# Half of a three-tap filter moved from TensorE to ScalarE and VectorE in a projection stage

## The reference, cut to what matters

```python
q = silu(causal_dwconv(x @ Wq, conv_q))      # 4 taps per channel
k = silu(causal_dwconv(x @ Wk, conv_k))
v = silu(causal_dwconv(x @ Wv, conv_v))
fs = fir(v, fir_short)                       # 3 taps per channel, causal
fl = fir(v, fir_long)                        # 31 taps
```

## Time and profile before

| what | value |
|---|---|
| median of three runs | 2584.63 us |
| lowest, highest | 2580.68, 2588.43 us |
| span of the profiled execution | 2587.5 us |
| the stage `conv_heads` in it | 117 to 442.7 us |
| TensorE, records of matmuls, whole span | 2394.4 us, 93% |
| VectorE, whole span | 1655.0 us, 64% |
| ScalarE, whole span | 1109.5 us, 43% |

### The profile page before, as it was taken

One profiled execution on the slowest core, in us unless ns is written; L12 is line 12 of the kernel. 1 busy time (PEld: TensorE's weight loads), 2 busy tenths in 40 slices (PEclk: granted clock), 3 DMA queues, 4 the chain that ended last, 5 costly groups with the idle time before them and its releaser, 6 DMA issues.

```text
span 2587.5 us, 41994 instructions
## 1 busy us (share of the span) xinstructions
PE 2394.4 (93%) x14594; PEld 1659.7 (64%) x14594; DVE 1655.0 (64%) x4354; ACT 1109.5 (43%) x2350; POOL 616.3 (24%) x417
## 2 busy tenths in 40 slices
PE   6899997667897999979999999999999999999998
PEld 4466665555676888845666666666666666666665
DVE  4487886449922566525767676667667676766675
ACT  2477876346663222224334424433443344244331
POOL 1145554031101111211312231222123132312210
PEclk9999998787667999989999999999999999999999
DMA  5447556978767767421202210220122022101000
GB/s 166 162 149 219 174 166 192 270 212 203 212 155 223 217 204 225 156 74 49 58 1 58 58 50 9 58 58 13 45 59 58 1 58 58 43 15 58 9 9 8
DMA packets 376312, 272.14 MB, mean 105 GB/s; under 512 B 199714, under 2 KB 333794, under 8 KB 373906
## 3 DMA queue, kind: packets, MB, share of 16 engines
q1 hardware_dynamic: 371474, 243.85, 33.6%
q0 software_dynamic: 4640, 25.73, 2.9%
HBM read 168.60 MB, written 100.93 MB: 104 GB/s over the span
## 4 chain that ended last, share of the span: by engine, by line
PE 43%; DVE 9%; issue 3%; POOL 2%; ACT 0%; DMA 0%; DVEq 0%; SPq 0%; POOLq 0%; ACTq 0%
PE mx_dn L2002 16%; PE mx_up L1988 15%; PE mx_m L1938 4%; DVE mx_acc L2316 4%; PE mx_m L1965 2%; POOL mx_rms L1894 2%; PE mx_m L1942 1%; PE mx_m L1979 1%; DVE hl L2224 1%; DVE mx_st L2214 1%; DVE hl L2199 1%; DVE hl L2188 1%; DVE mx_rms L2193 1%; PE mx_m L1973 1%; PE mx_m L1947 1%
## 5 line engine op out<-in xcount | busy, mean ns | idle before, releaser
L2316 DVE SCALAR_TENSOR_TENSOR mx_acc<-mx_dn,mx_comb,mx_acc 128x256 f32<-128x256 f32 x1024 | 424.3, 478 | 356.6 <-PE mx_dn L2002 352.7
L2002 PE MATMUL mx_dn<-mx_edn,mx_hs 128*128 128x256 f32 x2048 | 487.7, 381 | 0.0
L1988 PE MATMUL mx_up<-mx_h2T,mx_eup 128*128 128x512 f32 x1024 | 484.3, 595 | 0.0
L2002 PEld LDWEIGHTS mx_dn<-mx_edn,mx_hs 128*128 128x128 f32 x2048 | 384.4, 190 | 145.6 <-issue 91.0
L2090 ACT ACTIVATE mx_hs<-mx_up 128x512 f32<-128x512 f32 x320 | 190.8, 596 | 625.8 <-PE mx_up L1988 625.1
L1988 PEld LDWEIGHTS mx_up<-mx_h2T,mx_eup 128*128 128x128 f32 x1024 | 190.9, 190 | 156.1 <-issue 145.2
L675 DVE SCALAR_TENSOR_TENSOR cv_acc<-cv_pre,conv_w,cv_acc 128x512 f32<-128x512 f32 x288 | 215.7, 750 | 78.2 <-ACT cv_acc L597 71.3
L539 PE MATMUL cv_pj<-cv_hT,wqkv 128*128 128x512 f32 x384 | 181.8, 604 | 12.7 <-ACT cv_acc L597 7.7
L713 POOL TENSOR_TENSOR rn<-cv_ss,half_pow 128x8 f32 x64 | 127.5, 1992 | 13.2 <-POOL cv_ss L709 13.2
L1880 POOL TENSOR_TENSOR mx_st<-mx_tmp,root_pow 128x24 f32<-128x24 f32 x30 | 124.6, 4168 | 20.1 <-DVE mx_tmp L2142 20.1
L1938 PE MATMUL mx_m<-mx_hT,wr 128*128 128x512 f32 x256 | 122.2, 601 | 3.3 <-DMA mx_x<-_attn_hidden_states_dram 2.5
(11 more groups left out here) (292 smaller groups left out, 3998.7 us busy)
## 6 DMA issues: line engine op xcount, KB each, us to landing
kqT_d<-cv_kqc SPq DMA_DIRECT2D x16, 1024.0 KB, 8.5
vf_d<-cv_vf SPq DMA_DIRECT2D x16, 1024.0 KB, 5.4
fl_toep<-taps_d SPq DMA_DIRECT2D x32, 392.0 KB, 7.3
ds_kqT<-kqT_d SPq DMA_DIRECT2D x10, 1024.0 KB, 5.9
fl_v<-vf_d SPq DMA_DIRECT2D x8, 1216.0 KB
ci_kT<-kqT_d POOLq DMA_DIRECT2D x19, 512.0 KB, 5.7
fl_d<-fl_out POOLq DMA_DIRECT2D x8, 1029.0 KB, 7.2
xin<-_attn_hidden_states_dram SPq DMA_DIRECT2D x16, 512.0 KB, 4.3
```

The lines of the kernel that those rows point to most:

```text
L1988: ins = pe.matmul(up_ps[x % 2][:], lhs, h2T[i][:, k, :], start=(k == 0), stop=(k == KD - 1))
L2002: ins = pe.matmul(dn_ps[(i + n) % 2][:, j, :], hs[x % 4][:, j * P:(j + 1) * P], rhs, start=(x == 0 and j % 2 == 0) or x >= NS, stop=(x >= ...
L2316: ins = dve.scalar_tensor_tensor(out=acc[i][:, j, :], in0=dn_ps[(i + n) % 2][:, j, :], scalar=comb[i][:, j, e:e + 1], in1=acc[i][:, j, :], ...
```

## The change

The short filter of channels 0 to 127 leaves PE. ACT multiplies the tile `vT[:, 0]` by the last tap into a new tile `fsT` (128x512), behind the last Silu of the unit and ahead of the halos. DVE adds the two other taps at the start of its `body`, ahead of the next unit's first block. PE's `turn_v` transposes the finished tile instead of doing three matmuls with the diagonal matrices, and its first turn of a unit waits for it, between the transposes of `vT` and that of `fsT`. Channels 128 to 255 stay as they were. There is one `fsT`, so ACT waits until PE has turned the unit before. The taps `fs_w` now live until the early stages end, and three semaphores are new.

```diff
@@ turn_v, on PE
+                if j == 0:
+                    pe.wait_ge(fsT_done, u + 1)
+                pe.transpose(vf_ps[j % 2][:, D:D + P], fsT[:, c0:c0 + P], m.ident[:])
-                for k in range(KD):
-                    for t in range(FIRS):
-                        ins = pe.matmul(vf_ps[j % 2][:, D + k * P:D + (k + 1) * P], vT[i][:, k, c0 + t:c0 + t + P],
-                                        m.diag_fs[:, k, t, :], start=(t == 0), stop=(t == FIRS - 1))
+                for t in range(FIRS):
+                    ins = pe.matmul(vf_ps[j % 2][:, D + P:2 * D], vT[i][:, 1, c0 + t:c0 + t + P], m.diag_fs[:, 1, t, :],
+                                    start=(t == 0), stop=(t == FIRS - 1))
@@ silu, on ACT
                 act.activation(dst, acc[o % 3][:], ACT.Silu).then_inc(silu_done, 1)
+                if o == NBLK - 1:
+                    act.wait_ge(silu_done, u * NBLK + (NBLK + 2))
+                    if not isinstance(u, int) or u:
+                        act.wait_ge(vf_done, u * J)
+                    act.activation(fsT[:], vT[i][:, 0, FIRS - 1:], ACT.Identity, scale=m.fs_w[:, 0, FIRS - 1:FIRS])\
+                        .then_inc(tap_done, 1)
@@ new, on DVE, and called first in body
+            def short(u, g):
+
+                i = g % 2
+                dve.wait_ge(tap_done, u + 1)
+                dve.wait_ge(vhalo_done, u + 1)
+                dve.scalar_tensor_tensor(out=fsT[:], in0=vT[i][:, 0, 1:1 + UT], scalar=m.fs_w[:, 0, 1:2], in1=fsT[:],
+                                         op0=ALU.mult, op1=ALU.add).then_inc(tap_step, 1)
+                dve.wait_ge(tap_step, u + 1)
+                dve.scalar_tensor_tensor(out=fsT[:], in0=vT[i][:, 0, 0:UT], scalar=m.fs_w[:, 0, 0:1], in1=fsT[:],
+                                         op0=ALU.mult, op1=ALU.add).then_inc(fsT_done, 1)
@@
             def body(u, g, nxt):
+                short(u, g)
                 for s in range(NBLK):
```

More of the change, by code:

```diff
@@ L56, in setup @@
         taus = sb("taus", [P, 8])
-        fs_w = sb("fs_w", [P, KD, FIRS])
+        fs_w = m.fs_w
         fl_w = sb("fl_w", [P, KD, FIRL])
@@ L454, in conv_heads @@
         vT = [sb(f"cv_vT{i}", [P, KD, FIRS - 1 + UT]) for i in two]
+        fsT = sb("cv_fsT", [P, UT])
         kqc = [sb(f"cv_kqc{i}", [P, 2 * KD, UT]) for i in two]
@@ L473, in conv_heads @@
         silu_done = sem("cv_silu_done")
+        tap_done = sem("cv_tap_done")
+        tap_step = sem("cv_tap_step")
+        fsT_done = sem("cv_fsT_done")
         vf_done = sem("cv_vf_done")
@@ L2417, in build @@
             m.wqkv = early.enter_context(nc.sbuf_tensor("wqkv", [P, KD, 3 * D], F32))
+            m.fs_w = early.enter_context(nc.sbuf_tensor("fs_w", [P, KD, FIRS], F32))
             for stage in EARLY:
```

## The result

The changed kernel takes 2603.31 us (median of 7 runs, 2595.71 to 2617.21), the kernel before 2586.35 us (7 runs). The ratio is 1.0066, with a 95% interval from 1.0041 to 1.0092: 17 us slower. The forecast was 2594.0, with a range from 2586 to 2607.

A forecast was written before the change was run, and what follows sets the result against it. The prediction took the ring between DVE and ACT, not PE, as the bound. 15 x 0.58 for ACT's tap less 4.2 gave +4.5 us, clock dips +4.8: +9.3, 2594.0 us, range 2586 to 2607.

The forecast's parts named there:

- The ring of DVE and ACT: Projections stage, unit boundary: DVE waits for ACT's scaled copy, ACT for DVE's last block; sets the period, pause 2.97 us.
- Rival 2: Projections stage: PE is the bound after all, so the kernel gets faster, -17 us, 2568; chance 0.06.
- rival 1: Projections stage: the clock holds everywhere, +4.5 us, 2589.1; chance 0.27.
- PE's relief: PE's lighter turns remove DVE's wait before the last block of a unit: 4.2 us back.
- ACT's tap: Inside the boundary pause, behind the last Silu: 0.58 us a boundary, at 15 boundaries.
- The tail: Stage's end: first turn some 2.2 us later, four turns 0.56 us shorter each; net 0, ends -1 and +1.
- DVE's taps: At the boundary, T+1.3 to T+2.85, inside the pause lasting to T+3.55: cost nothing, 0.7 us to spare.
- Rival 4: Unit boundary: DVE's taps aren't covered because the tap's chain is 0.7 late; +12 us, 2597; chance 0.09.
- PE's pause: First V turn of a unit: PE idles about 1.8 us ahead of the filtered tile, 2.9 of 3.3 us in all.
- The clock: PE's clock dips at 8 of 15 boundaries, 0.5 us each, plus 0.8 for half a longer dip: +4.8 us.
- rival 3: All 15 boundaries dip, a third of them twice as long: +20 us, 2605; chance 0.13.
- one sign of being wrong: The prediction counted itself wrong if, among other signs, another stage moved by over 2 us.

The follow-up runs named there:

- d_pehalf: Kernel before with PE's part of the change alone: one transpose for three filter matmuls, no ACT or DVE work, no wait; 2577.8 us, ratio 0.9956.
- a_fill: Changed kernel plus two idle-filling matmuls on PE in each unit's first V turn, ahead of the wait for the filtered tile; 2597.65 us, ratio 1.0025.
- c_nodve: Changed kernel without DVE's two taps, PE waiting for ACT's tap instead; 2590.55 us, ratio 1.0009.

## Why the prediction was right or wrong

Where the 15.7 us of the stage come from, by differences between profiles. The passages run from T of unit 0, the end of DVE's last block of it, to T of unit 15: 140.0 to 427.6 before, 141.0 to 425.6 in d_pehalf, 138.9 to 428.1 in a_fill, 141.0 to 444.4 after. The tail is what follows up to the long filter. Each kernel needed 19.5 us ahead of the passages.

| difference | 15 passages | tail | stage |
|---|---|---|---|
| PE's part alone (d_pehalf less before) | -3.0 | -2.0 | -5.1 |
| the taps and the wait for the filtered tile, clock held by the fillers (a_fill less d_pehalf) | +4.7 | +2.4 | +7.2 |
| the falls of the clock (the changed kernel less a_fill) | +14.1 | -0.5 | +13.6 |
| all | +15.8 | -0.1 | +15.7 |

The rows add up by construction; what each holds was forecast by itself. The two falls of d_pehalf, some 1.3 us in all, stand in the first row as a loss and in the second as a gain.

- **What bounds.** Right. The ring of DVE and ACT sets the period; 36 us taken from PE gave 5.1. Rival 2 is out, and so is rival 1, as the clock fell at 12 passages.
- **PE's relief.** Right. Forecast 4.2 in the passages; in the 13 of them in which the clock held before and in d_pehalf, 3.8 us were gained, some 4.3 for all 15.
- **ACT's tap.** Forecast 0.58 a passage, 8.7 in all; measured 0.42 on the average of the same 13 passages of d_pehalf and a_fill (5.5 us), some 6 for all 15. The next instruction did start 0.62 behind the tap, but 0.14 came back further on, between the second halo and the copy behind it (0.23 from start to start before, 0.09 after); why is not shown. The 0.5 us that a loop's end added to the ring also vanished under the tap.
- **The tail.** Right: forecast as 2.2 more for the later first turn and 2.2 less for the shorter turns. PE's part alone gave 2.0, the wait took it back, and the whole came to -0.1.
- **DVE's taps.** Right: T+1.3 to T+2.8, with 0.57 to spare, and c_nodve shows the same pause without them (3.42 us). Rival 4 is out.
- **PE's pause.** Right in place: 1.75 us, forecast as 1.8. The idle time ahead of the transposes of `vT` was forecast as 1.1 everywhere; it was 1.06 where the unit before had no fall and 0.37 where it had one, as the last kq turn then ended at T+0.35 and not at T-0.4. So eight of the 12 falls came behind 2.1 us of idle time and not the 2.9 that the forecast worked with.
- **The clock.** The mechanism was right and its size was not: +4.8 forecast, +14.1 measured in the passages (+13.6 in the stage). This is the term that failed, twice. I took 8 passages with a fall; there were 12. And I priced one at 0.5 us by ACT's wait for one kq turn alone; most cost 1.0. The third block started 0.67 late against the unit without a fall, and ACT, which has next to no slack in a slot, came late to the fourth block as well, by 0.31 more (0.59 and 0.23 of idle time on DVE). The two long ones cost 2.2 and 2.3, close to the 2.1 priced (0.5 and 1.6), and there were two where half of one was counted. The ten others cost 0.8 to 1.0. The end of the range, rival 3 (+20 us), was nearer to the truth than the forecast, but partly by luck: it had 15 falls at too low a price and five long ones.
- **By the sum.** 4.5 + 4.8 = 9.3 against 2.1 + 13.6 = 15.7: the first term was 2.4 too high, the second 8.8 too low. The direction was right, and the result lies inside the range because the range was drawn around rival 3.
- **Two readings beside the sum.** The profiled execution before was not the slowest of the three: each run on record lies some 1.7 us above its own span (2599.86 for 2598.1), which puts it near 2589.2, above all three times. Nothing in the sum hangs on it. And one sign of being wrong did come, another stage that moves by over 2 us: the mixing was 4.1 us shorter and the long filter 2.1. Since the mixing also differs by 4.2 us between the two executions of a_fill, that says nothing against the ring; for the long filter no run shows the reason.

## What to carry to other kernels

When work is moved off an engine that looks full, ask first what sets the period, and then what the moved work's wait does to the engine that was relieved: here the lighter TensorE waited in one piece of 1.75 us, its clock fell in 12 of 15 passages, and the half-speed stretch hit the next deadline. Start the moved work where the engines already stand (ACT's idle time ahead of the last Silu), so that its result is there before it is asked for. A filler of idle matmuls is a cheap test that tells a clock loss from a work loss.

## What the runs showed that was not expected

- The clock falls behind pauses that are not whole: 0.37, 0.18 and 1.02 us of idle with transposes and six matmuls between them were enough at seven passages of c_nodve.
- A pause of one and the same size goes with a fall or without. In the changed kernel all four boundaries with 2.7 to 2.8 us of idle time went with a fall, but only eight of the eleven with 2.1 (0.37 and 1.75 ahead of 266 with a fall, 0.38 and 1.75 ahead of 306 without). What decides there is not shown.
- The falls repeat from one execution to the next: the changed kernel's 15 passages were the same in both profiles, kind by kind, within 0.1 us.
- The delta scan took 287.2 and 296.5 us in two executions of one and the same kernel, with the clock's late return in the longer one (c_nodve has 289 us, in between). What decides the length was not tried.
